# Two rows of probabilities masked at once, and seven kinds of small work handed from VectorE to GpSimd

## Chip, cores and metric

The kernel runs on one core of one Trainium2 chip. The metric is the device time of one execution in microseconds; below, that is the median of three runs. The engines are named as in the profile: PE is TensorE's matmul, PEld its weight load, DVE is VectorE, ACT is ScalarE, POOL is GpSimd, SP is SyncE, which here only issues DMAs.

## What is computed

A transformer layer in float32: x is 8 batches of 1024 rows of 128 features. After a layer norm comes attention with 8 heads of 16 features and relative positions, whose scores are shifted, and then a router with eight experts, two per token. Cut to what matters here:

```python
content = jnp.einsum('bqhd,bkhd->bhqk', q + u_bias, k)
pos_score = jnp.einsum('bqhd,khd->bhqk', q + v_bias, p)
pos_score = _rel_shift(pos_score)          # pad one column, reshape, drop the first row
score = (content + pos_score) / jnp.sqrt(jnp.float32(e))
attn = jax.nn.softmax(score, axis=-1)
ctx = jnp.einsum('bhqk,bkhd->bqhd', attn, v).reshape(b, s, e)
x = x + ctx @ Wo + bo
...
router_logits = jnp.einsum('bsk,ke->bse', h, Wr2) + br2     # then top 2 of 8 experts
output = output + y * expert_mask[:, :, e][:, :, None]      # for each expert
```

The shift makes three kinds of score for a query row and a key column. On and below the diagonal one set of operands holds ("lower", QL), from two above the diagonal on another ("upper", QU), and on the super-diagonal, one above, the position part is absent. So a 128x128 block on the diagonal is a mixture.

## The kernel before, in words

The kernel has a prologue (to about 88 us), a loop over the eight batches of attention and routing (to about 1233), an end of the routing, and then the experts (from about 1312). The change touches the loop and what leads to it; of the experts only the name of one tensor's slice.

**The loop.** A batch is 8 heads of 9 units, u = 0 to 8; (h, u) names head and unit. Every engine has its own program of the same 72 units, written out by hand, and waits on counting semaphores of the others. In a unit PE does two halves of the second pass of head h (scores of one block row of 128 keys by 1024 queries, into pB, L677) and two pieces of the first pass of head h + 2 (scores into the three banks of pA, L655), which VectorE reads to find the maxima (L1083, L1089). ScalarE takes the exponentials of pB (L985, L987): at u = 0 into `upper_diag`, the diagonal blocks computed with the upper operands, at u > 0 into `prob`, a ring of four rows, kb = u - 1. GpSimd masks (L555 to L575): at u = 0 the eight upper blocks at once; at each u > 0 it sets one element to zero (L568), keeps the lower triangle of the diagonal block (L570) and adds the upper block (L575), and then counts `p_mask` by one. PE's `context` (L698) waits for that count; it runs for two rows at a time, at units 4, 6 and 8 for rows 0 to 5 and at unit 1 of the next head for rows 6 and 7.

**Work between the units.** Tables such as `LOW_AT` name the unit at which a piece of other work is done. Float32 operands are split into a high half, rounded, and a low half, the rest; c, k, gl and gu are the operands, each in two pieces of 512 columns, for the next batch. ScalarE makes the high halves, VectorE the low ones (`low`, L1062), each counted in `low_done`. gu is read from PSUM, c, k and gl from SBUF. SyncE stores them to DRAM at heads 2, 3 and 4 (`store`, L291). `maxima` (L1093) ends a head on VectorE: it reduces the maxima to `mneg` and makes `dsup`, the difference on the super-diagonal, of which ScalarE takes the exponential at the head's end (L1029). The other small work on VectorE's path in this text is the normalization of the values (`vsh`, L1117 to L1127, head 0), the router's rows (L1155, L1158, units 0, 1, 3 and 4 of head 3, transposed by PE at L748) and its hidden layer (`hr`, L1182, units 1 and 2 of head 5, transposed by PE at L760, the "fold"). GpSimd has besides the masks the position products (L482 to L491), reciprocal roots (L453 to L469, L505, L507), the residual's bias (L497) and the indirect DMAs that scatter routed rows (L517).

**Order.** Nothing is planned by a program: each engine's queue is in the order of its code, and these tables set where the small work stands in it. The mask's core is

```python
if kb > 0:
    po.memset(prob[kb % RING][0:1, P * kb - 1:P * kb], 0.0)
p = prob[kb % RING][:, P * kb:P * kb + P]
po.affine_select(out=p, in_=p, compare_op=ALU.is_ge, fill=0.0, base=0,
                 pattern=[[1, P]], channel_multiplier=-1).then_inc(lower_masked, 1)
```

Of the kernel before, what the change touches and what calls it, by code (L numbers as in the profile page):

```python
# [21 lines left out]
P = 128  # L22
# [47 lines left out]
def attention_phase(nc, dram, keep):  # L70

    ctx = ExitStack()
    with ctx:
# [36 lines left out]
        prob = [keep["b2"]] + [sb(f"prob{i}", [P, S]) for i in range(1, RING)]  # L110
# [50 lines left out]
        ln, low_done, pos, norm, rs_done, res_done = (sem(n) for n in ("ln", "low_done", "positions", "norm", "rs_done", "residual_biased"))  # L161
# [12 lines left out]
        LN_N, LOW_N, POS_N, NORM_N, HI_N, RS_N = 3 * NB, 8, 8, 6, 8, 9  # L174
# [23 lines left out]
        LOW_AT = {(1, 2): 0, (2, 3): 1, (2, 7): 2, (3, 2): 3, (3, 6): 4, (4, 1): 5, (4, 3): 6, (4, 4): 7}  # L198
        POSITIONS_AT = ((1, 1), (1, 4), (1, 8), (2, 1), (2, 4), (2, 6), (5, 4), (5, 6))
# [4 lines left out]
        RESIDUAL_AT, LAST_HEADS_AT, FIRST_HEADS_AT = ((7, 1), (7, 4)), (0, 6), (6, 4)  # L204
# [4 lines left out]
        SCATTER_AT = ((0, 1), (0, 4), (0, 6), (0, 8), (1, 6), (3, 1), (3, 6), (3, 8), (4, 4), (4, 6), (5, 1), (5, 8), (6, 1), (6, 4), (6, 6), (6, 8))  # L209
# [44 lines left out]
        def _(sp):  # L254
# [145 lines left out]
            sp.dma_start(keep["b2"][:, :], dram["b2"].partition_broadcast(P)).then_inc(d_big, 16)  # L400
# [14 lines left out]
        def _(po):  # L415
# [5 lines left out]
            for i in range(1, RING):  # L421
                po.memset(prob[i][:, :], 1.0).then_inc(set_pool, 1)
# [69 lines left out]

            def residual(b, half):
# [40 lines left out]
            for i in range(RS_N):  # L534
# [15 lines left out]
                             pattern=[[1, P]], channel_multiplier=-1).then_inc(set_r, 1)  # L550
            po.wait_ge(m_done, 1)
# [491 lines left out]
        def _(v):  # L1043
# [255 lines left out]
            for n in range(4, LOW_N):  # L1299
                low(0, n)  # L1300
# [452 lines left out]
```

## Time and profile before

| | us |
|---|---|
| median of three runs | 1685.92 |
| lowest, highest run | 1685.19, 1691.73 |
| the profiled execution, as a run | 1683.95 |
| its span in the trace | 1682.2 |

The rows further down come from this one execution. Their times are microseconds from the span's start. "xN" is a count, "idle before" or a bracket at a row's end is the time for which the engine did nothing before the instruction and what released it. Matmuls are pipelined and their ends are modelled: a row of PE of 0.40 us does not mean that the next cannot start after 0.23. Weight loads (PEld) run ahead of their matmuls. `b_all` in a row is the ring's first row, which lies in the tensor of an expert bias (`b2`).

### The profile page before, as it was taken

What the parts mean: (1) busy time and instruction counts of PE and PEld (TensorE: products, weight loads), DVE (VectorE), ACT (ScalarE), POOL (GpSimd) and SP (SyncE); (2) the same over time, 40 slices, a digit from 0 to 9 for tenths busy, and PEclk for the clock granted to TensorE, in tenths of its full rate; (3) what the DMA queues carried; (4) which work ended last, traced back from release to release, by engine and by line L of the source; (5) the groups of instructions that cost most, each with busy time, mean ns of one, the idle gap of its engine ahead of it and who ended that gap; (6) DMA issues with size and microseconds to landing.
All of it is one profiled execution on the core that took longest, in us unless ns stands there. A gap on an engine that the chain in (4) does not pass through costs nothing. (4 is left out here: it accounts for less than half of the span.)

```text
span 1682.2 us, 51020 instructions
## 1 busy us (share of the span) xinstructions
PE 1549.5 (92%) x12534; PEld 1207.6 (72%) x12535; DVE 1402.2 (83%) x5272; ACT 1113.2 (66%) x2303; POOL 1106.0 (66%) x2090
## 2 busy tenths in 40 slices
PE   3789999999999999999999999999951799999997
PEld 1567777677676767777767776767731799999997
DVE  4669899989989987998998998899854588888886
ACT  2157776776777776677777777767730577777775
POOL 5257767767766775776677677677663276666666
PEclk8689999999999998999999999999975899999999
DMA  5746535535644553464364355346454243443433
GB/s 136 198 116 177 145 94 156 163 93 130 183 111 122 163 155 85 104 198 108 104 185 136 96 160 164 97 122 189 113 147 127 43 59 52 56 57 51 57 53 48
DMA packets 134404, 199.99 MB, mean 119 GB/s; under 512 B 20936, under 2 KB 95576, under 8 KB 134192
## 3 DMA queue, kind: packets, MB, share of 16 engines
q1 hardware_dynamic: 108336, 177.21, 39.1%
q0 software_dynamic: 25856, 20.27, 7.8%
q8 instruction: 94, 1.54, 0.4%
q14 instruction: 118, 0.97, 0.2%
HBM read 108.24 MB, written 75.33 MB: 109 GB/s over the span
## 5 line engine op out<-in xcount | busy, mean ns | idle before, releaser
L1083 DVE CUSTOM_DVE_ANT_0 junk<-pA,lmask 128x512 bf16<-128x512 f32 x1056 | 686.8, 682 | 63.1 <-PE pA L670 44.1
L985 ACT ACTIVATE prob<-pB 128x512 f32<-128x512 f32 x384 | 229.9, 599 | 204.5 <-PE pB L689 115.8
L1576 POOL DMA_INDIRECT out<-yb,dst x144 | 230.9, 1604 | 134.9 <-ACT yb L1650 82.5
L691 PE MATMUL pB<-QL,K 97*128 97x512 f32 (+3 forms) x768 | 285.7, 372 | 1.4 <-ACT upper_diag L985 1.4
L668 PE MATMUL pA<-K,QL 96*128 96x512 f32 (+3 forms) x792 | 281.8, 357 | 5.0 <-DMA K<-split_operands 3.2
L689 PE MATMUL pB<-QU,K 97*128 97x512 f32 (+3 forms) x640 | 267.1, 417 | 0.3
L670 PE MATMUL pA<-K,QU 96*128 96x512 f32 (+3 forms) x660 | 233.1, 354 | 4.5 <-DVE acc L1083 3.2
L987 ACT ACTIVATE prob<-pB 128x512 f32<-128x512 f32 x384 | 227.8, 593 | 12.7 <-PE pB L691 4.5
L707 PE MATMUL pC<-prob,vext 128*17 128x256 f32 x3088 | 217.4, 384 | 0.1
L575 POOL TENSOR_TENSOR prob<-prob,upper_diag 128x128 f32<-128x128 f32 x384 | 180.2, 469 | 32.0
L689 PEld LDWEIGHTS pB<-QU,K 97*128 97x128 f32 x640 | 121.9, 190 | 99.4 <-issue 59.3
L517 POOL DMA_INDIRECT routed_rows<-sent,sent_to x144 | 157.9, 1097 | 29.9 <-issue 25.6
L568 POOL MEMSET prob<- 1x1 f32 x384 | 34.0, 89 | 203.9 <-ACT prob L987 202.6
L668 PEld LDWEIGHTS pA<-K,QL 96*128 96x128 f32 x792 | 153.5, 194 | 13.8 <-DVE acc L1083 4.4
L1089 DVE CUSTOM_DVE_ANT_0 junk<-pA,umask 128x128 bf16<-128x128 f32 x528 | 122.1, 284 | 43.8 <-PE pA L674 41.3
L691 PEld LDWEIGHTS pB<-QL,K 97*128 97x128 f32 x768 | 147.1, 192 | 15.8 <-ACT upper_diag L985 3.3
L1689 DVE SCALAR_TENSOR_TENSOR g<-pLin,b_all,gl 128x256 f32<-128x256 f32 x292 | 127.5, 478 | 22.6 <-PE pLin L1599 14.5
L670 PEld LDWEIGHTS pA<-K,QU 96*128 96x128 f32 x660 | 128.0, 194 | 22.2 <-DVE acc L1083 14.9
L1605 PE MATMUL pY<-w_all,g 128*128 x1152 | 140.3, 275 | 0.0
L707 PEld LDWEIGHTS pC<-prob,vext 128*17 128x17 f32 x3088 | 78.1, 97 | 84.0 <-issue 22.3
L1605 PEld LDWEIGHTS pY<-w_all,g 128*128 128x128 f32 x1152 | 135.0, 192 | 0.0
L1643 ACT ACTIVATE gl<-pGate,b_all 128x256 f32<-128x256 f32 x292 | 121.0, 465 | 13.1 <-PE pGate L1599 12.2
(305 smaller groups left out, 3656.5 us busy)
## 6 DMA issues: line engine op xcount, KB each, us to landing
QL<-split_operands SPq DMA_DIRECT2D x67, 256.0 KB, 3.7
QU<-split_operands SPq DMA_DIRECT2D x67, 256.0 KB, 4.1
K<-split_operands SPq DMA_DIRECT2D x67, 256.0 KB, 4.4
xg<-routed_rows SPq DMA_DIRECT2D x76, 132.0 KB
split_operands<-c_h SPq DMA_DIRECT2D x36, 256.0 KB, 6.1
split_operands<-c_l SPq DMA_DIRECT2D x36, 256.0 KB, 6.4
QL<-split_operands SPq DMA_DIRECT2D x67, 128.0 KB, 3.6
QU<-split_operands SPq DMA_DIRECT2D x67, 128.0 KB, 4.1
```

Of the source, the lines that this page charges most:

```text
L517: po.indirect_dma_start(dram["xs"], bass.IndirectOffsetOnAxis(sent_to[:, t, j:j + 1], 0), sent[:, t, :], None).then_inc(scattered, 16)
L575: po.tensor_tensor(p, p, upper_diag[h % 2][:, P * kb:P * kb + P], ALU.add).then_inc(p_mask, 1)
L668: mm = pe.matmul(dst[:, 0:low], QL[0:KROWS, s, q], K[0:KROWS, s, k0:k0 + low], start=True, stop=True)
L670: mm = pe.matmul(dst[:, low:HALF], QU[0:KROWS, s, q], K[0:KROWS, s, k0 + low:k0 + HALF], start=True, stop=True)
L689: mm = pe.matmul(pB[:, q0:q0 + up], K[0:r, s, k], QU[0:r, s, q0:q0 + up], start=True, stop=True)
L691: mm = pe.matmul(pB[:, q0 + up:q0 + HALF], K[0:r, s, k], QL[0:r, s, q0 + up:q0 + HALF], start=True, stop=True)
L707: mm = pe.matmul(pC[VW * strip:VW * strip + D + 1, :], vext[:, kb, h % H, :], prob[kb % RING][:, quarter * strip:quarter * strip + quarter ...
L985: act.activation(p[:, 0:HALF], pB[:, 0:HALF], ACT.Exp, scale=SCALE).then_inc(p_exp, 1)
L987: act.activation(p[:, HALF:S], pB[:, HALF:S], ACT.Exp, scale=SCALE).then_inc(p_exp, 1)
L1083: v.tensor_tensor_reduce(out, src[:, :], lmask[:, at:at + HALF], 1.0, -3.0e38, ALU.add, ALU.max, acc[:, s, qb, n % 2:n % 2 + 1]).then_inc( ...
L1576: po.indirect_dma_start(dram["out"], bass.IndirectOffsetOnAxis(dst[k][:, a:a + 1], 0), yb[k][:, a, :], None, compute_op=ALU.add).then_inc( ...
L1605: mm = pe.matmul(pY[k % 2][:, a, :], g[k % 2][:, c, P * a:P * a + P], keep["w2"][:, bass.ds(ex * F + c * E, E)], start=(c == 0), stop=(c = ...
```

## The change

The ring of four rows becomes two tensors of two rows each. GpSimd no longer masks a row at every unit u > 0, but two rows at the even units: one select over both diagonal blocks and one addition over both, and `p_mask` rises by two. Six of the eight low halves per batch (c, k and gl) and the eight differences `dsup` move from VectorE to GpSimd; the two of gu, which lie in PSUM, stay, with a semaphore of their own (`gu_low`). The differences stand at unit 3 of the head before. Positions, scatters and a residual move by a unit or so, mostly to odd units. VectorE waits for all eight differences before it overwrites the super-diagonal's scores, and PE for the six low halves before it projects into their sources.

```diff
-        prob = [keep["b2"]] + [sb(f"prob{i}", [P, S]) for i in range(1, RING)]
+        ring = [keep["b2"], sb("prob23", [P, 2, S])]
+        prob = [ring[i // 2][:, i % 2, :] for i in range(RING)]
...
-        LOW_AT = {(1, 2): 0, (2, 3): 1, (2, 7): 2, (3, 2): 3, (3, 6): 4, (4, 1): 5, (4, 3): 6, (4, 4): 7}
+        LOW_AT = {(3, 6): 4, (4, 4): 7}
+        SPLIT_AT = {(0, 3): 0, (1, 8): 1, (2, 8): 2, (3, 3): 3, (3, 7): 5, (4, 2): 6}
+        DSUP_AT = 3
...
-                sp.wait_ge(low_done, lows)
+                sp.wait_ge(gu_low if name == "gu" else low_done, lows)
...
+            def low(nb, n):
+
+                name, half = SPLITS[n]
+                cut = slice(HALF * half, HALF * half + HALF)
+                src = {"c": qu, "k": kc, "gl": g_lo}[name][:, cut]
+                have = known(po, nb * HI_N + n + 1)
+                po.wait_ge(set_pool, POOL_SET)
+                po.wait_ge(hi_done, have)
+                po.tensor_tensor(parts[name][1][:, cut], src, parts[name][0][:, cut].bitcast(F32), ALU.subtract).then_inc(low_done, 1)
+
+            def super_difference(b, h):
+
+                s = h % H
+                have = known(po, b * H + h + 1)
+                po.wait_ge(set_pool, POOL_SET)
+                po.wait_ge(mx_done, have)
+                po.tensor_tensor(dsup[:, s, :], acc[:, s, :, 3], mneg[:, s, :].bitcast(F32), ALU.add).then_inc(dsup_done, 1)
...
-                        else:
-                            kb = u - 1
-                            if kb > 0:
-                                po.memset(prob[kb % RING][0:1, P * kb - 1:P * kb], 0.0)
-                            p = prob[kb % RING][:, P * kb:P * kb + P]
+                        elif u % 2 == 0:
+                            kb = u - 2
+                            both_rows = ring[kb // 2 % 2][:, :, :].rearrange("p a s -> p (a s)")
+                            for k in (kb, kb + 1)[kb == 0:]:
+                                po.memset(prob[k % RING][0:1, P * k - 1:P * k], 0.0)
+                            p = both_rows.rearrange("p (n q) -> p n q", q=P)[:, kb:kb + NB + 2:NB + 1, :]
                             po.affine_select(out=p, in_=p, compare_op=ALU.is_ge, fill=0.0, base=0,
-                                             pattern=[[1, P]], channel_multiplier=-1).then_inc(lower_masked, 1)
+                                             pattern=[[0, 2], [1, P]], channel_multiplier=-1).then_inc(lower_masked, 1)
...
-                            po.tensor_tensor(p, p, upper_diag[h % 2][:, P * kb:P * kb + P], ALU.add).then_inc(p_mask, 1)
+                            po.tensor_tensor(p, p, upper_diag[h % 2][:, P * kb:P * kb + 2 * P].rearrange("p (n q) -> p n q", q=P), ALU.add).then_inc(p_mask, 2)
+                        if u == DSUP_AT:
+                            super_difference(b, h + 1)
+                        if (h, u) in SPLIT_AT:
+                            low(b + 1, SPLIT_AT[h, u])
...
+                                    pe.wait_ge(low_done, (b + 1) * LOW_N + LOW_N)
...
-                v.wait_ge(mx_done, b * H + h + 1)
-                v.tensor_tensor(dsup[:, s, :], acc[:, s, :, 3], mneg[:, s, :].bitcast(F32), ALU.add).then_inc(dsup_done, 1)
...
                 elif name == "super":
+                    v.wait_ge(dsup_done, b * H + H)
                     super_out(src, done)
```

How this moves instructions is best seen in the queues. First GpSimd, from the end of head 2 to the start of head 3: `prob` and `b_all` are rows of the ring, `rs_r` the router's reciprocal root, `upper_diag` the upper blocks. Before:

```order
L575 TENSOR_TENSOR prob<-prob,upper_diag 128x128
L62 ISA
L505 TENSOR_SCALAR rs_r<-mv_r 128x8
L507 TENSOR_TENSOR rs_r<-rs_r,mhalf 128x8
L62 ISA
L568 MEMSET prob 1x1
L570 AFFINE_SELECT prob<-prob 128x128
L572 REGISTER_ALU
L575 TENSOR_TENSOR prob<-prob,upper_diag 128x128
L62 ISA
L563 AFFINE_SELECT upper_diag<-upper_diag 128x1024
```

and with the change:

```order
L602 TENSOR_TENSOR b_all<-b_all,upper_diag 128x2x128
L62 ISA x2
L530 TENSOR_SCALAR rs_r<-mv_r 128x8
L532 TENSOR_TENSOR rs_r<-rs_r,mhalf 128x8
L62 ISA
L595 MEMSET prob 1x1 x2
L597 AFFINE_SELECT prob<-prob 128x2x128
L599 REGISTER_ALU
L602 TENSOR_TENSOR prob<-prob,upper_diag 128x2x128
L508 TENSOR_TENSOR k_l<-kc,k_h 128x512
L62 ISA
L589 AFFINE_SELECT upper_diag<-upper_diag 128x1024
```

The mask of the seventh row no longer stands ahead of the root, and the first low half of k now stands between the last mask and the select of the next head's upper blocks.

Second VectorE, around unit 2 of head 3: `junk` with `lmask` is the read of a score bank. Before:

```order
L62 REGISTER_ALU
L1083 ISA junk,acc<-pA,lmask 128x512
L1083 ISA acc 128x1
L1067 REGISTER_ALU
L1068 TENSOR_TENSOR k_l<-kc,k_h 128x512
L62 REGISTER_ALU
L1083 ISA junk,acc<-pA,lmask 128x512
L1083 ISA acc 128x1
L62 REGISTER_ALU
L1083 ISA junk,acc<-pA,lmask 128x512
L1083 ISA acc 128x1
L1158 SCALAR_TENSOR_TENSOR rows_r<-xres,mv_r,rs_r 128x128 x2
```

and with the change:

```order
L62 REGISTER_ALU
L1116 ISA junk,acc<-pA,lmask 128x512
L1116 ISA acc 128x1
L62 REGISTER_ALU
L1116 ISA junk,acc<-pA,lmask 128x512
L1116 ISA acc 128x1
L62 REGISTER_ALU
L1116 ISA junk,acc<-pA,lmask 128x512
L1116 ISA acc 128x1
L1189 SCALAR_TENSOR_TENSOR rows_r<-xres,mv_r,rs_r 128x128 x2
```

The low half of k is gone from between the reads, and the router's third step stands right behind them.

Third GpSimd at units 3 and 4 of head 0. Before, with the ring's rows numbered:

```order
L62 ISA
L568 MEMSET prob2 1x1
L570 AFFINE_SELECT prob2<-prob2 128x128
L572 REGISTER_ALU
L575 TENSOR_TENSOR prob2<-prob2,upper_diag0 128x128
L62 ISA
L568 MEMSET prob3 1x1
L570 AFFINE_SELECT prob3<-prob3 128x128
L572 REGISTER_ALU
L575 TENSOR_TENSOR prob3<-prob3,upper_diag0 128x128
L517 DMA routed_rows<-sent,sent_to 67584x132
```

and with the change:

```order
L516 TENSOR_TENSOR dsup<-acc,mneg 128x8
L62 ISA
L508 TENSOR_TENSOR c_l<-qu,c_h 128x512
L62 ISA
L595 MEMSET prob23 1x1 x2
L597 AFFINE_SELECT prob23<-prob23 128x2x128
L599 REGISTER_ALU
L602 TENSOR_TENSOR prob23<-prob23,upper_diag0 128x2x128
```

A difference and the first low half of c take the place of a mask at unit 3, the pair is masked at unit 4, and the scatter behind it has moved to unit 5.

## Rows read from the trace of the kernel before

**Rows 1.** The page: busy time, share of the span and instructions.

```profile
PE 1549.5 (92%) x12534; PEld 1207.6 (72%) x12535; DVE 1402.2 (83%) x5272; ACT 1113.2 (66%) x2303; POOL 1106.0 (66%) x2090
```

**Rows 2.** Windows: stretch, length, busy of five engines (instructions), TensorE clock, DMA share, GB/s.

```profile
797.70:939.20 141.50, 139.99 (x1159) 100.25 (x1157) 129.08 (x530) 103.87 (x211) 100.68 (x232) 1.00 0.49 136
...
630.00:635.00 5.00, 5.00 (x31) 4.25 (x29) 3.26 (x15) 3.00 (x7) 2.60 (x7) 0.82 0.26 69
635.00:640.00 5.00, 5.00 (x28) 3.19 (x28) 2.97 (x19) 2.07 (x4) 2.26 (x7) 0.50 0.04 14
```

**Rows 3.** Waits of weight loads, 797.7 to 939.2: us in total, times, longest.

```profile
PEld pM L760 <- DVE hr L1182: 1.4, 1, 1.4
PEld pA L670 <- DVE acc L1083: 1.1, 3, 0.5
...
PEld pM L748 <- DVE rows_r L1158: 0.7, 1, 0.7
...
PEld pM L734 <- DVE vsh L1127: 0.3, 1, 0.3
PEld pA L668 <- DVE acc L1083: 0.3, 1, 0.3
```

**Rows 4.** Timeline, batch 5: start, us, instruction, count, idle before and releaser.

```profile
833.65 0.19 PEld L668 LDWEIGHTS pA<-K,QL 96*128 96x128 f32 x1 [0.30 <-DVE acc L1083]
...
867.38 0.20 PEld L748 LDWEIGHTS pM<-ident_f,rows_r 128*128 128x128 f32 x2 [0.20 <-issue]
...
872.13 0.42 PEld L748 LDWEIGHTS pM<-ident_f,rows_r 128*128 128x128 f32 x4 [0.72 <-DVE rows_r L1158]
...
904.08 0.42 PEld L760 LDWEIGHTS pM<-ident_f,hr 128*128 128x128 f32 x4 [1.35 <-DVE hr L1182]
```

**Rows 5.** VectorE's lines that move: ns minimum/median/maximum, first and last start.

```profile
L1068 DVE TENSOR_TENSOR c_l<-qu,c_h x18: 677/810/991, 30.2 to 1134.6; 128x512 fp32r<-128x512 f32 x18
L1068 DVE TENSOR_TENSOR k_l<-kc,k_h x18: 673/676/686, 31.6 to 1150.7; 128x512 fp32r<-128x512 f32 x18
L1068 DVE TENSOR_TENSOR gl_l<-g_lo,gl_h x18: 673/682/689, 41.1 to 1169.3; 128x512 fp32r<-128x512 f32 x18
...
L1099 DVE TENSOR_TENSOR dsup<-acc,mneg x66: 166/189/650, 71.2 to 1233.1; 128x8 f32<-128x8 f32 x66
```

**Rows 6.** GpSimd's nearest forms, from the answers on single lines, as above.

```profile
L570 POOL TENSOR_SCALAR_AFFINE_SELECT prob<-prob x384: 282/293/819, 99.7 to 1232.5; 128x128 f32<-128x128 f32 x192
...
L575 POOL TENSOR_TENSOR prob<-prob,upper_diag x384: 453/458/1332, 100.1 to 1232.9; 128x128 f32<-128x128 f32 x192
...
L491 POOL TENSOR_TENSOR g_lo<-g_lo,t x18: 1259/1282/1287, 35.2 to 1140.4; 128x512 f32<-128x512 f32 x18
```

**Rows 7.** Timeline around the start of head 3: GpSimd, then VectorE, then PE.

```profile
859.08 0.88 POOL L575 TENSOR_TENSOR prob<-prob,upper_diag 128x128 f32<-128x128 f32 x1
...
860.38 1.67 POOL L507 TENSOR_TENSOR rs_r<-rs_r,mhalf 128x8 f32<-128x8 f32 x1
...
862.43 0.46 POOL L575 TENSOR_TENSOR prob<-prob,upper_diag 128x128 f32<-128x128 f32 x1
862.84 1.10 POOL L563 TENSOR_SCALAR_AFFINE_SELECT upper_diag<-upper_diag 128x1024 f32<-128x1024 f32 x1
...
862.88 1.09 DVE L1155 TENSOR_SCALAR rows_r<-rows_r 128x8 f32<-128x8 f32 x1
863.88 0.71 DVE L1158 SCALAR_TENSOR_TENSOR rows_r<-xres,mv_r,rs_r 128x128 f32<-128x128 f32 x2
...
863.19 1.06 PE L707 MATMUL pC<-prob,vext 128*17 128x256 f32 x16
```

**Rows 8.** Timeline, head 0 of the same batch: VectorE and GpSimd.

```profile
812.23 1.22 DVE L1117 TENSOR_TENSOR vsh<-vsh,psup 128x1024 f32<-128x1024 f32 x1
...
812.42 1.35 POOL L575 TENSOR_TENSOR b_all<-b_all,upper_diag 128x128 f32<-128x128 f32 x1 [0.17 <-POOL b_all L570]
...
817.55 1.29 DVE L1119 TENSOR_TENSOR vsh<-vsh,ctx_all 128x896 f32<-128x896 f32 x1
```

More of the change, by code:

```diff
@@ L160, in attention_phase @@
         e_ready, e_done, hi_done = sem("e_ready"), sem("e_done"), sem("hi_done")
-        ln, low_done, pos, norm, rs_done, res_done = (sem(n) for n in ("ln", "low_done", "positions", "norm", "rs_done", "residual_biased"))
+        ln, low_done, gu_low, pos, norm, rs_done, res_done = (sem(n) for n in ("ln", "low_done", "upper_low", "positions", "norm", "rs_done", "residual_biased"))
         placed, moved = sem("head_values_placed"), sem("values_shifted")
@@ L171, in attention_phase @@
         block = ctx.enter_context(nc.Block())
-        LN_N, LOW_N, POS_N, NORM_N, HI_N, RS_N = 3 * NB, 8, 8, 6, 8, 9
+        LN_N, LOW_N, GU_N, POS_N, NORM_N, HI_N, RS_N = 3 * NB, 6, 2, 8, 6, 8, 9
         E_AT = [1, 2, 4, 6, 7, 8, 9, 10]
@@ L229, in attention_phase @@
         READY = {"c": 2, "k": 4, "gl": 7, "gu": 8}
+        LOWS = {"c": 2, "k": 4, "gl": 6}
         PAIRS_AT = {1: (-1, 6), 4: (0, 0), 6: (0, 2), 8: (0, 4)}
@@ L315, in _ @@
                 sp.wait_ge(hi_done, READY[name])
-                sp.wait_ge(low_done, READY[name])
+                if name == "gu":
+                    sp.wait_ge(gu_low, GU_N)
+                else:
+                    sp.wait_ge(low_done, LOWS[name])
                 store_side(name, 0)
@@ L399, in _ @@
             sp.dma_start(keep["b1"][:, :], dram["b1"]).then_inc(d_big, 16)
[L400 removed]
+            sp.dma_start(keep["b2"][:, 0, :], dram["b2"].partition_broadcast(P)).then_inc(d_big, 16)
             sp.wait_ge(w_done, B * W_N + 2)
@@ L421, in _ @@
             for i in range(1, RING):
-                po.memset(prob[i][:, :], 1.0).then_inc(set_pool, 1)
+                po.memset(prob[i], 1.0).then_inc(set_pool, 1)
             po.memset(mhalf[:, :], -0.5).then_inc(set_pool, 1)
@@ L550, in _ @@
                              pattern=[[1, P]], channel_multiplier=-1).then_inc(set_r, 1)
+            super_difference(0, 0)
             po.wait_ge(m_done, 1)
@@ L723, in _ @@
             pe.wait_ge(low_done, LOW_N)
+            pe.wait_ge(gu_low, GU_N)
             for h in range(AHEAD):
@@ L787, in small_piece @@
                 elif part == 0 and name == "values 0":
-                    pe.wait_ge(low_done, (b + 1) * LOW_N + LOW_N)
+                    pe.wait_ge(gu_low, (b + 1) * GU_N + GU_N)
                 elif part == 0:
@@ L848, in _ @@
                                 else:
-                                    pe.wait_ge(low_done, (b + 1) * LOW_N + SPLITS.index(("gu", 0)) + 1)
+                                    pe.wait_ge(gu_low, (b + 1) * GU_N + 1)
                                 upper_form(half, pE, 0, 2)
@@ L1298, in _ @@
                 stats(1, t)
-            for n in range(4, LOW_N):
+            for n in range(4, HI_N):
                 low(0, n)
@@ L1712, in step @@
                 v.wait_ge(down, i + 1)
-                v.tensor_tensor(yb[k][:, :, :], pY[k % 2][:, :, :], keep["b2"][:, bass.ds(step.experts[k] * E, E)].unsqueeze(1).to_broadcast([P, HALVES, E]), ALU.add).then_inc(y_done, 1)
+                v.tensor_tensor(yb[k][:, :, :], pY[k % 2][:, :, :], keep["b2"][:, 0, bass.ds(step.experts[k] * E, E)].unsqueeze(1).to_broadcast([P, HALVES, E]), ALU.add).then_inc(y_done, 1)
             ex = load_experts(mybir.EngineType.DVE, 0, 2)
```

14 lines of the change are left out of this document (7 added, 7 removed).

## The prediction, as it was put on record

> **What bounds the kernel now.** I read the page's busy line first, then one batch of the loop by window, then who waited for whom in that batch, then single stretches of the timeline. The page says PE 92%, VectorE 83%, GpSimd 66% [rows 1]. The change touches only the eight-batch loop, so one batch has to be read: batch 5, from 797.70 to 939.20 us, 141.50 us long, with VectorE busy 129.08, PE 139.99, ScalarE 103.87 and GpSimd 100.68 us at full TensorE clock [rows 2]. The next batch is as long to the hundredth; one row stands for all.
>
> VectorE at 91% looks like the bound, and then every microsecond taken from it would be a microsecond of time. The waits say otherwise. Weight loads run just ahead of their matmuls, so idle time before a weight load is the plainest sign that PE is held up. In the whole batch VectorE held weight loads up for 1.4 (router fold), 1.1 and 0.3 (score banks not yet read), 0.7 (router rows) and 0.3 (values): 3.8 us of 141.5, seven times [rows 3]. Elsewhere PE goes on with its own queue, or plays ping-pong with ScalarE's exponentials, whatever VectorE does. So VectorE has a backlog in places, three score banks deep, which mostly costs nothing. **The change can give back at most those 3.8 us per batch, and only those whose backlog contains a removed instruction.**
>
> **What is taken from VectorE.** Per batch two low halves each of c (810 ns median), k (676) and gl (682), and eight differences of 189 ns [rows 5]: 2 x (0.81 + 0.68 + 0.68) + 8 x 0.19 = 5.9 us, 47 us in eight batches. Now each held-up place:
> - Head 1, the score bank at 833.65, held up 0.30 [rows 4]. Two units ahead of it VectorE did a low half of c (up to 991 ns [rows 5]), with no idle time from there to the read that frees the bank. That goes. The wait can lose 0 to 0.30; I take 0.15, since a load also idles for its issue.
> - Head 3, router rows at 872.13, held up 0.72 [rows 4]. The low half of k at head 3, unit 2, stands two router steps ahead of it. It is worth 0.68, more than the wait beyond the 0.20 that the same line idles where it waits for nothing (867.38) [rows 4]. Gain 0.52.
> - Head 5, router fold at 904.08, held up 1.35 [rows 4]. VectorE works without a gap from the end of head 4; of its work there only one difference goes. Gain 0.19.
> - The other four (two more banks in head 3, one in head 2, the normalized values at the start of head 1) stand before a removed low half, or behind an idle gap of VectorE that swallows the removed difference: 0.
> - The low halves of gl in head 4 and the second of c and the first of k in head 2 stand where nobody waits: 0.
>
> Relief: 0.15 + 0.52 + 0.19 = 0.86 us per batch, **6.9 us in eight** (bounds: 0 if other backlogs move in; 8 x 1.01 = 8.1 if the 0.30 goes whole).
>
> **What GpSimd gets.** A fused mask covers 2 x 128 columns. The trace has no such form; the nearest rows are select 0.29 us for 128 columns and 1.10 for 1024, addition 0.46 for 128 and 1.28 for 512 [rows 6, 7]. By straight lines between them, an estimate: 0.40 and 0.73. A pair cost 2 x (0.29 + 0.46) = 1.50 and now costs 1.13, so four pairs and eight heads save 0.37 x 32 = 11.8 us per batch, less a little for the access pattern. The six low halves cost 6 x 1.28 = 7.7 by the same 128x512 addition, the eight differences between 0 and 8 x 0.46 = 3.7. So GpSimd stays at about 100 us of 141.5: load is no danger.
>
> Latency could be. A pair is masked only once its second row is there, and then takes 0.38 longer than one row did (1.13 against 0.75). The contexts consume a pair two units later, and the scarcest place I found in the batch is head 3, unit 1: mask done at 862.89, contexts at 863.19, 0.30 to spare [rows 7]. There the new order is no later: the row masked ahead of the root (0.88 for its addition alone) goes, so the root's power starts near 859.1 instead of 860.38 and the pair is done near 862.1. Elsewhere the pair has 0.6 us or more. I take 0; once, at the loop's very end, 0.4 us. The moved positions, scatters and the residual now lie mostly at odd units, which have no mask any more: hidden in that room. New waits on PE and VectorE (the differences before the super-diagonal is overwritten, the low halves before the projection) are met three units or more ahead: 0. SyncE's stores of c, k and gl wait for GpSimd's halves one or two units later than for VectorE's, but are needed heads later: 0.
>
> **What the two engines do to each other** is the cost I cannot read straight off. An addition of GpSimd that is 458 ns in the median took 1.35 us at 812.42, beside a two-input VectorE operation of 1.22 us from 812.23 [rows 6, 8]. In the other direction a 128x8 step of VectorE took 1.09 us at 862.88, beside a 1.10 us select of GpSimd from 862.84 [rows 7], and the low half of c ranges from 677 to 991 ns [rows 5]. So they do not overlap freely: the later one waits. Not always, though: at 863.88 two VectorE steps took 0.71 us beside GpSimd work, nearly undelayed [rows 7]. The Trainium skill says more sharply (SBUF — State Buffer, section "Who interferes with whom") that a VectorE instruction with two SBUF inputs and a GpSimd instruction that reads SBUF exclude each other for the whole of whichever came first. By that rule the trace agrees in its long overlaps and not in this short one.
>
> Two places are exposed. Head 3, unit 0: by the durations above GpSimd would do pair, low half of k (862.1 to 863.4) and then the select (to 864.5), where the router step of 863.88 ended at 864.59. That step could end up to 0.6 later, and the two bank waits of head 3 behind it are without slack. Head 0, unit 4: the VectorE operation at 817.55 [rows 8] meets the pair's addition of 0.73, where it met one of 0.46; it may win or lose by a tenth, 0 to 0.7, and VectorE has no gap from there to the values that ScalarE and PE wait for. Bounds: 0 to 1.3 per batch. I take 0.3, near the lower end, as the short overlaps of the trace cost 0.1 to 0.2 each: **+2.4 us in eight**.
>
> **Sum.** -6.9 + 2.4 + 0.4 = -4.1 us. The profiled execution took 1683.95, so 1679.9; the median of the runs lies 1.97 above it (1685.92), so 1681.8 us, 0.24% less.
>
> **The rivals.**
> A. *VectorE is the bound after all.* For it: 91% busy, and PE's 99% proves little, since the ends of its matmuls are modelled. The Trainium skill (Perfetto Trace Analysis, section "Identifying the Most-Contended Engine") ranks engines by occupancy and takes VectorE's as a fair measure, but PE's only by its weight loads; by that rule VectorE would come first here. Against it: 3.8 us of held-up loads. Then all 47 us come back: 1639. Chance 0.05.
> B. *Relief without a price.* GpSimd's operations fall beside single-input work of VectorE, and ScalarE's ping-pong gains a little too. 1685.92 - 8.1 + 0.4 = 1678.2; and the traced execution has one stretch at half clock within the loop (granted 0.82 over 630 to 635 and 0.50 over 635 to 640, which is 1.2 GHz, though PE shows no idle time in either [rows 2]), some 13 us long, which cost at most half of that; without it 6 us less, 1672. Chance 0.25 for under 1677.5.
> C. *The port takes more than it gives.* Each low half holds VectorE's two-input work at head 0 and head 3, 1.3 us per batch, and the relief of 0.86 is used up by the same delay, which reaches the router rows: 1685.92 + 8 x 1.3 + 0.4 = 1696.7. It ends slower once the two places cost more than the relief by 1 us per batch. For it: overlaps of 0.9 us in the rows; against: GpSimd may well start before VectorE arrives, and the trace's usual overlaps cost little. Chance 0.15, counting milder forms joined by a second stretch at half clock.
> D. The forecast, 1677.5 to 1694: chance 0.55.
>
> **How the numbers follow.** The range should reach from B's lower value to the milder part of C: 1671 to 1693. What lies beyond is A and the whole of C, about 0.2. Half a per cent, 8.4 us, is about what a measurement of this kernel can tell from no change: faster 0.30 (A and B), within 0.55, slower 0.15.
>
> **What would show it.** In the profile after: VectorE's busy time in a batch near 123 us, GpSimd's near 100, and the batch near 141.0. The held-up load of the router rows gone, that of the fold near 1.15, the bank waits of head 3 unchanged or up to 0.6 longer. VectorE's idle time before score banks grows by some 6 us per batch: that is where the freed time goes. Wrong if the batch is under 139 (then backlog counted everywhere), if the fused select or addition takes over 1 us, or if contexts wait for GpSimd by more than 0.4 anywhere.

## The result, and the profile after

The changed kernel is slower: 1703.89 us (median of 5 runs, 1699.0 to 1706.83) against 1690.35 for the kernel before (5 runs beside them and earlier, 1685.19 to 1693.68), ratio 1.0086, 95% interval 1.0063 to 1.0108. The profiled execution took 1706.2 us, 22.3 more than that of before. Its page:

```profile
PE 1560.8 (92%) x12534; PEld 1213.0 (71%) x12535; DVE 1370.5 (80%) x5158; ACT 1113.4 (65%) x2303; POOL 1074.7 (63%) x1691
```

VectorE has lost 32 us of busy time and GpSimd 31 against [rows 1], and PE needed 11 more. So work was saved on both engines and time was lost. Windows of one batch, cut at VectorE's maxima so that each is one head (stretch, length, busy of PE, weight loads, VectorE, ScalarE, GpSimd, granted clock, DMA share, GB/s): heads 0, 3, 4, 6 and the whole, first of before (batch of [rows 2], cut 10.6 us later), then of after.

```profile
808.33:826.59 18.26, 18.26 (x148) 13.22 (x146) 17.10 (x57) 13.06 (x27) 13.19 (x29) 1.00 0.48 125
...
860.89:878.74 17.85, 17.45 (x140) 11.88 (x139) 16.84 (x62) 13.51 (x26) 13.64 (x33) 1.00 0.66 199
878.74:897.80 19.06, 19.04 (x164) 14.24 (x161) 16.66 (x71) 13.25 (x29) 14.50 (x35) 1.00 0.64 185
...
914.63:933.80 19.17, 19.17 (x170) 14.74 (x166) 15.91 (x82) 13.87 (x29) 12.82 (x30) 1.00 0.34 90
...
808.33:949.88 141.55, 140.04 (x1160) 100.25 (x1158) 129.14 (x529) 103.92 (x212) 100.73 (x231) 1.00 0.49 136
```

```profile
820.62:839.44 18.82, 18.50 (x146) 13.10 (x145) 17.37 (x57) 12.92 (x26) 13.08 (x23) 1.00 0.46 125
...
873.08:891.74 18.66, 17.79 (x144) 12.30 (x142) 17.09 (x61) 13.67 (x28) 15.08 (x30) 1.00 0.65 198
891.74:911.12 19.38, 19.14 (x163) 14.24 (x161) 15.18 (x69) 13.25 (x29) 13.16 (x28) 1.00 0.60 178
...
928.00:947.58 19.58, 19.58 (x168) 14.84 (x166) 16.06 (x81) 14.17 (x30) 11.10 (x23) 1.00 0.33 87
...
820.62:963.66 143.04, 140.14 (x1159) 100.23 (x1158) 125.34 (x516) 103.94 (x211) 96.38 (x181) 1.00 0.49 135
```

A batch is 1.5 us longer, 12 in eight, in four heads; the undisturbed batches of before lie between 141.43 and 141.58 us, those of after between 142.99 and 143.10, which makes a batch's length a far finer measure than the whole time. In heads 0 and 3 VectorE is busier than before although instructions were taken away there: its busy time holds waiting. The weight loads held up by VectorE in that batch (us, times, longest) answer to [rows 3]:

```profile
PEld pM L792 <- DVE hr L1213: 1.5, 1, 1.5
...
PEld pA L699 <- DVE acc L1116: 0.8, 2, 0.4
PEld pA L701 <- DVE acc L1116: 0.8, 1, 0.8
...
PEld pM L780 <- DVE rows_r L1189: 0.6, 1, 0.6
PEld pM L766 <- DVE vsh L1158: 0.6, 1, 0.6
PEld pM L805 <- DVE both L1249: 0.4, 1, 0.4
```

Sum 4.7. The same count for before gives 4.0: the prediction's 3.8 left out one wait of 0.2 for `both` (L1218). GpSimd's new operations cost what was estimated (groups by form: busy us, mean ns; the mean of an addition holds its waiting, its median is 0.73 us):

```profile
L602 POOL TENSOR_TENSOR prob<-prob,upper_diag 128x256 f32<-128x256 f32 x128 | 99.8, 780 | 19.0
...
L597 POOL TENSOR_SCALAR_AFFINE_SELECT prob<-prob 128x256 f32<-128x256 f32 x128 | 52.3, 408 | 0.0
...
L508 POOL TENSOR_TENSOR c_l<-qu,c_h 128x512 fp32r<-128x512 f32 x16 | 20.6, 1285 | 0.0
...
L516 POOL TENSOR_TENSOR dsup<-acc,mneg 128x8 f32<-128x8 f32 x65 | 13.7, 211 | 42.5 <-DVE mneg L1130 24.2 <-ACT prob L1020 17.6
```

The rest of the 22.3 us lies in stretches at half clock (2.8 in the last batch), in batch 0 (2.0), ahead of the loop (2.6), behind it (2.1) and in the experts (0.5). The two stretches outside the loop look like chance: kernels with the same prologue as the changed one reached the loop's start between 82.0 and 87.0 us (before 83.4, after 86.0), and the end part took 79.6 to 83.6 us over fourteen traces (before 81.5, after 83.6, the longest).

### The profile page after: what moved, and what is told of

Same layout as the page of the kernel before. It is cut to its first block and busy times, and to the rows that moved or that the text cites. A ratio compares the mean times of both kernels' runs of the same rounds, so it can differ in the third digit from the quotient of the medians.

```text
span 1704.5 us, 50588 instructions
## 1 busy us (share of the span) xinstructions
PE 1560.8 (92%) x12534; PEld 1213.0 (71%) x12535; DVE 1370.5 (80%) x5158; ACT 1113.4 (65%) x2303; POOL 1074.7 (63%) x1691
## 5 line engine op out<-in xcount | busy, mean ns | idle before, releaser
L1608 POOL DMA_INDIRECT out<-yb,dst x144 | 235.6, 1636 | 130.7 <-ACT yb L1682 77.1
L1018 ACT ACTIVATE b_all<-pB 128x512 f32<-128x512 f32 x256 | 153.1, 598 | 146.8 <-PE pB L720 81.4
L1018 ACT ACTIVATE prob<-pB 128x512 f32<-128x512 f32 x256 | 153.4, 599 | 115.8 <-PE pB L720 61.7
L1020 ACT ACTIVATE prob<-pB 128x512 f32<-128x512 f32 x256 | 151.8, 593 | 9.6 <-PE pB L722 4.2
L1020 ACT ACTIVATE b_all<-pB 128x512 f32<-128x512 f32 x256 | 152.1, 594 | 4.9 <-PE pB L722 1.7
L738 PE MATMUL pC<-prob,vext 128*17 128x256 f32 x2064 | 138.2, 386 | 1.0 <-POOL prob L602 1.0
L738 PE MATMUL pC<-b_all,vext 128*17 128x256 f32 x2048 | 138.0, 388 | 0.9 <-POOL b_all L602 0.9
```

Of the source, the lines that this page charges most:

```text
L738: mm = pe.matmul(pC[VW * strip:VW * strip + D + 1, :], vext[:, kb, h % H, :], prob[kb % RING][:, quarter * strip:quarter * strip + quarter ...
L1018: act.activation(p[:, 0:HALF], pB[:, 0:HALF], ACT.Exp, scale=SCALE).then_inc(p_exp, 1)
L1020: act.activation(p[:, HALF:S], pB[:, HALF:S], ACT.Exp, scale=SCALE).then_inc(p_exp, 1)
L1608: po.indirect_dma_start(dram["out"], bass.IndirectOffsetOnAxis(dst[k][:, a:a + 1], 0), yb[k][:, a, :], None, compute_op=ALU.add).then_inc( ...
```

## Where each piece of it is

Timeline (start, us, instruction). Head 0, unit 6, the addition of the last head's values on VectorE and GpSimd's mask beside it, before and after:

```profile
821.77 0.31 DVE L1121 TENSOR_TENSOR vsh<-vsh,ctx_all 128x128 f32<-128x128 f32 x1
...
821.47 0.46 POOL L575 TENSOR_TENSOR prob<-prob,upper_diag 128x128 f32<-128x128 f32 x1
```

```profile
833.92 0.79 DVE L1152 TENSOR_TENSOR vsh<-vsh,ctx_all 128x128 f32<-128x128 f32 x1
...
833.83 0.73 POOL L602 TENSOR_TENSOR b_all<-b_all,upper_diag 128x256 f32<-128x256 f32 x1
```

Both end 0.15 after GpSimd's addition: 821.93 to 822.08 before, 834.56 to 834.71 after. The fused addition is longer, so the wait is. It happens again at unit 8:

```profile
837.91 1.61 DVE L1158 TENSOR_TENSOR vsh<-vsh,den 128x1024 f32<-128x1024 f32 x1
...
837.71 0.73 POOL L602 TENSOR_TENSOR prob<-prob,upper_diag 128x256 f32<-128x256 f32 x1
```

Head 3: the low half of k (874.75 to 876.04) holds the first router step, and pushes the select behind it onto the next two, which last 1.51 together where the same two took 0.71 [rows 7]:

```profile
875.46 0.61 DVE L1186 TENSOR_SCALAR rows_r<-rows_r 128x8 f32<-128x8 f32 x1
875.99 1.51 DVE L1189 SCALAR_TENSOR_TENSOR rows_r<-xres,mv_r,rs_r 128x128 f32<-128x128 f32 x2
...
874.75 1.29 POOL L508 TENSOR_TENSOR k_l<-kc,k_h 128x512 fp32r<-128x512 f32 x1
876.00 1.10 POOL L589 TENSOR_SCALAR_AFFINE_SELECT upper_diag<-upper_diag 128x1024 f32<-128x1024 f32 x1
```

Head 6, end: a copy of 8 columns, 0.21 us before, ends with GpSimd's addition (947.18):

```profile
946.50 0.71 DVE L1245 COPY rows_r<-xf 128x8 f32<-128x8 f32 x1
...
946.45 0.73 POOL L602 TENSOR_TENSOR prob<-prob,upper_diag 128x256 f32<-128x256 f32 x1
```

Head 4 looked like more of the same, a scatter in the way, and was not (below). The working theory P: each instruction of GpSimd holds a VectorE instruction that needs the same access until it ends. Rival L: masks and differences come later, contexts or exponentials wait. Later came C: breaks in VectorE's own supply of instructions, seen as an instruction that starts late although its wait is met and no other engine holds it.

## The experiments

Each head is the third smallest of its seven lengths (batch 0 left out), so that stretches at half clock drop out (for head 6 of e5 and e10 the second smallest); sum is their sum. Head 0 of e5, e10 and e12 does not repeat as the others do (19.00 to 19.51, 19.13 to 19.78 and 18.57 to 19.19 us), so their sums are low by some tenths. Ratio is the whole time against the kernel before on the same chip.

| kernel | h0 | h1 | h2 | h3 | h4 | h5 | h6 | h7 | sum | ratio, 95% |
|---|---|---|---|---|---|---|---|---|---|---|
| before | 18.26 | 18.00 | 16.27 | 17.85 | 19.05 | 16.80 | 19.16 | 16.08 | 141.5 | |
| after | 18.81 | 17.77 | 15.86 | 18.64 | 19.38 | 16.87 | 19.58 | 16.07 | 143.0 | 1.0063 to 1.0108 |
| e1 | 18.17 | 17.77 | 15.89 | 18.61 | 19.42 | 16.89 | 19.62 | 16.07 | 142.4 | 1.0025 to 1.0072 |
| e2 | 18.81 | 17.78 | 15.89 | 17.69 | 19.42 | 16.88 | 19.62 | 16.07 | 142.2 | 1.0016 to 1.0065 |
| e3 | 18.81 | 17.77 | 15.86 | 18.63 | 19.39 | 16.88 | 19.58 | 16.07 | 143.0 | 1.0036 to 1.0080 |
| e4 | 18.17 | 17.77 | 15.86 | 17.69 | 19.39 | 16.88 | 19.45 | 16.08 | 141.3 | 0.9977 to 1.0010 |
| e5 | 19.17 | 17.77 | 15.89 | 17.68 | 19.07 | 17.19 | 19.18 | 16.09 | 142.0 | 1.0038 to 1.0086 |
| e6 | 18.81 | 17.76 | 16.79 | 17.35 | 19.06 | 16.94 | 19.64 | 16.07 | 142.4 | 1.0029 to 1.0077 |
| e7 | 18.35 | 17.78 | 15.87 | 19.23 | 19.38 | 16.63 | 19.45 | 15.95 | 142.6 | 1.0032 to 1.0071 |
| e8 | 18.26 | 17.77 | 15.89 | 17.41 | 19.06 | 16.78 | 19.16 | 16.08 | 140.4 | 0.9868 to 0.9939 |
| e9 | 18.17 | 17.76 | 15.86 | 17.68 | 19.37 | 16.88 | 19.21 | 16.22 | 141.2 | 0.9987 to 1.0043 |
| e10 | 19.30 | 17.78 | 15.87 | 17.69 | 19.40 | 17.18 | 19.14 | 16.08 | 142.4 | a single run |
| e11 | 18.17 | 17.76 | 15.86 | 17.67 | 19.02 | 16.89 | 19.21 | 16.22 | 140.8 | 0.9945 to 0.9971 |
| e12 | 18.62 | 18.00 | 16.27 | 18.17 | 19.04 | 16.61 | 19.19 | 16.45 | 142.3 | 0.9999 to 1.0030 |

**e1.** Two of the 32 pairs masked row by row again, with a select and an addition of 128 columns each, as before the change:

```diff
+        SINGLE_AT = ((0, 6), (0, 8))
...
+                        elif (h, u + u % 2) in SINGLE_AT:
+                            kb = u - 1
...
```

> The changed kernel, but the two last pairs of rows of head 0 (units 5 to 8) are masked row by row as before; all other pairs stay fused. Theory P (GpSimd's longer addition holds VectorE's two-input steps): in the changed kernel the addition of values at unit 6 of head 0 waits for a fused addition of 0.73 us (0.79 us instead of 0.31), and the last one at unit 8 for another (1.61 instead of 1.36). Both go back, PE's held-up score bank at the end of head 0 (+0.36) and the late values at the start of head 1 (+0.27) with them: a batch 143.0 -> 142.3 us, the whole 5 to 6 us less than the changed kernel. Theory L (the loss is latency: contexts or exponentials wait for the later masks or for GpSimd's queue): two of 32 pairs matter little, at most 0.1 us per batch.

Head 0 fell 0.64, no other moved by more than 0.04. P stands for head 0; L doesn't.

**e2.** `-(2, 8): 2, (3, 3): 3` `+(3, 3): 3, (3, 5): 2` in SPLIT_AT.

> The changed kernel, but GpSimd makes the first low half of k at unit 5 of head 3, not at unit 8 of head 2, so that the select of the upper blocks is not pushed back by 1.28 us. Theory P: the router step at the start of head 3 lasts 0.45 us again, not 1.25, and the two score banks behind it come 0.3 and 0.25 us earlier: a batch 143.0 -> 142.5. Theory L: no more than 0.1, since nobody waits for the low half of k. If something at units 5 and 6 of head 3 is hit instead, the batch stays at 143.0 and the new delay shows there.

Head 3 fell 0.95, almost twice what was expected. P again.

**e3.** `-(3, 5), (4, 5), (4, 7)` `+(3, 5), (4, 4), (4, 7)` in SCATTER_AT.

> The changed kernel, but one of the sixteen scatters, that of head 4, unit 5, is issued at unit 4, as before the change. Theory P, widened to GpSimd's indirect DMAs: in the changed kernel the four short score reads of unit 6 in head 4 start 0.44 us after their wait is over, just as the scatter ends, and PE is held up 0.36 us at unit 8; that goes: a batch 143.0 -> 142.65. Theory L or chance: the batch stays within 0.1 us of 143.0.

Nothing moved: head 4 keeps its 19.39, and the late reads with it, with GpSimd idle beside them. P widened to scatters fails: the scatter had only stood there.

**e4.** e1, e2 and e3 together, SINGLE_AT with (6, 8) too.

> The changed kernel with all three repairs, and the last pair of head 6 masked row by row too (there a copy of the router's choice lasted 0.71 us instead of 0.21 beside the fused addition, 0.29 us late at head 7). Theory P: 143.0 - 0.7 - 0.5 - 0.35 - 0.3 = 141.15 us per batch, below the kernel before (141.48) by the 0.3 us of relief, and the whole about 15 us under the changed kernel, 0 to 3 us under the kernel before. Theory L: 142.5 or more per batch.

141.3 instead of 141.15: heads 0 and 3 add up, head 6 gave only 0.13, head 4 nothing. The whole is level with the kernel before, as the batch says (-0.17 x 8 = -1.4 us).

**e5.** e4, and in VectorE's loop:

```diff
+                        if (h, u) == (1, 6):
+                            for _ in range(20):
+                                v.wait_ge(set_dve, DVE_SET)
```

> The kernel with all repairs (141.31 us per batch), with 20 waits that are always met (0.02 us each) put into VectorE's program at head 1, unit 6, where it idles 0.8 us: as many instructions as the change took out of VectorE's program ahead of head 4. What stayed late in all variants, the short score reads of head 4, unit 6 (they start 0.44 us after their wait is met, with GpSimd idle; 0.08 elsewhere), hits always the same instruction, 491st of the 871 of the loop. Theory C (a break in VectorE's supply of instructions, at a fixed distance in its program): the break moves to another instruction and head 4 lasts 19.05 us again, as before the change: 141.31 -> 140.95, unless the new place is as bad. Theory S (something that head 4 itself does, whatever stands ahead): nothing moves, 141.3.

Ten more instructions stand in the loop (881 for 871; waits are paired). Head 4 fell to 19.07, three heads further on than the padding: theory C. But head 0 rose by 1.0 and head 5 by 0.3, and the sum is 142.0. Head 0 is a break behind the loop's branch (e12). Head 5 is a small break that lets GpSimd go first: a short read comes 0.15 us late, the fused addition starts at 915.25, 0.07 ahead of VectorE's step with `rq`, and that step lasts 1.21 us; in e4 the step started 0.11 ahead of the addition and lasted 0.69, and the addition waited.

**e6.** SPLIT_AT empty, all eight lows in VectorE's LOW_AT, the differences back in `maxima`.

> The changed kernel with the six low halves and the eight differences back on VectorE at their old places: of the change only the fused masks and the moved positions, scatters and residual are left. Theory P: the fused addition costs 0.55 at head 0 and about 0.3 at head 6 by itself, so with no relief left a batch is 141.48 + 0.9 = 142.4, and GpSimd is busy only about 88 us of it. Theory L (GpSimd's queue and its added work delay the masks): the cost came with the added work, so 141.5 or less.

142.4 as expected by P, with VectorE busy 130 us and GpSimd only 89. The fused masks cost 0.55 at head 0; of the 0.48 at head 6 about half belongs to a moved scatter (e9). Head 2 is 0.5 longer, which was not expected, and it is P again, this time by a moved position product of GpSimd that meets the low half of c left on VectorE (0.75 us before the change in the same batch):

```profile
853.73 1.62 DVE L1098 TENSOR_TENSOR c_l<-qu,c_h 128x512 fp32r<-128x512 f32 x1
...
853.52 1.28 POOL L498 TENSOR_TENSOR g_lo<-g_lo,t 128x512 f32<-128x512 f32 x1
```

Head 3 is 0.5 shorter: the mask of the seventh row no longer stands ahead of the select of the upper blocks, the select starts 0.4 us earlier in the head, and the router steps wait less for it.

**e7.** SINGLE_AT holds all 32 pairs.

> The changed kernel with all rows masked one by one as before: of the change the low halves and differences on GpSimd and the moved tables are left. GpSimd then has about 108 of 143 us busy. Theory P: without the fused additions 0.55 and 0.3 go, the delay by the low half of k (0.8) and the late reads of head 4 (0.36) stay: 142.1. Theory L: GpSimd's queue is longer than in the changed kernel, so contexts wait: 143.5 or more.

142.6: between the two. Heads 0 and 6 behave as P says, and head 5 falls by 0.24, since an addition of 128 columns holds a step of `hr` for 0.47 us instead of 0.75. Head 3 is 0.6 worse than in the changed kernel: masks one by one shift GpSimd's queue, and the second low half of k now meets a router step (the first of the two below lasts 1.28):

```profile
872.28 1.54 DVE L1205 SCALAR_TENSOR_TENSOR rows_r<-xres,mv_r,rs_r 128x128 f32<-128x128 f32 x2
...
872.13 1.28 POOL L510 TENSOR_TENSOR k_l<-kc,k_h 128x512 fp32r<-128x512 f32 x1
```

GpSimd is busy 107.7 us of it, and no head but the third is longer than in the changed kernel: its load alone costs nothing that shows.

**e8.** In the kernel before:

```diff
-                cut = slice(HALF * half, HALF * half + HALF)
+                cut = slice(HALF * half, HALF * half + (HALF if isinstance(nb, int) or name == "gu" else 8))
```

> The kernel before, with the six low halves of c, k and gl cut to 8 columns inside the loop (0.1 us instead of 0.7 to 0.8; the rest of the computation of these halves is left out): the relief alone, with nothing put on GpSimd. The prediction's terms for it: 0.15 at head 1 and 0.52 at head 3, 141.48 -> 140.8. Theory N (VectorE's backlog hides it all, the freed time turns into idle time ahead of the next score bank): 141.4. Theory V (VectorE is the bound): 4 us less, 137.5.

140.4: the relief by six low halves is 1.05 us per batch, 0.23 in head 1, 0.38 in head 2, 0.44 in head 3. V is far off, N too. The profiled execution is 12.0 us shorter than that of before: 8.4 by the batches, 6.2 by a stretch of 13.7 us at half clock that is missing (batch 3 of before 147.71, its neighbours 141.48), less 1.5 each for two stretches of 3.4 us. The ratio of the runs says 16 us; what makes the rest is not shown.

**e9.** `SPLIT_AT = {(0, 3): 0, (1, 8): 1, (3, 5): 2, (3, 7): 3, (4, 1): 5, (4, 2): 6}`, SINGLE_AT as e4, scatter (6, 7) to (6, 8).

> The changed kernel with the two last pairs of head 0 and the last of head 6 masked row by row, and moved on GpSimd: both low halves of k to head 3, units 5 and 7, behind the router steps of that head (the first low half of gl follows at head 4, unit 1), and the scatter of head 6, unit 7, to unit 8, behind the mask that it holds up in the repaired kernel. Theory P: head 3 lasts 17.41 us as in the kernel with short low halves, not 17.69, and head 6 lasts 19.16 as before the change, not 19.44: 141.31 -> 140.75 us per batch, 0.7 below the kernel before, 6 us in eight. If the two-input steps of other places are hit by the moved low halves: 141.3 or more.

Head 6 came as expected (19.21). Head 3 did not move: the second low half of k had held nobody. Why e8's head 3 is 0.27 shorter is seen in e11 below. The whole time does not show the gain: the interval holds 1, and the runs reach from 1679.8 to 1702.8 us.

**e10.** e5's padding at (4, 7) instead of (1, 6).

> The kernel with all repairs, with the same 20 waits that are always met (10 instructions in the trace), but at head 4, unit 7, behind the late reads. Theory C (breaks in VectorE's supply of instructions at fixed distances in its program): the instructions up to head 4 stand where they stood, so the reads of head 4, unit 6 are late again (19.4 us for head 4, where 10 instructions ahead of them gave 19.07), and what comes behind them, head 5 (17.19 instead of 16.88) and head 6 (20.4 instead of 19.44), is as with the other padding. Theory S: head 4 as with the other padding or all as without.

Head 4 is 19.40 again, head 5 as with the other padding, and head 0 long again (19.30): C, since nothing but the position differs. Head 6 is 19.14 and not 20.4: that expectation had taken a stretch at half clock in e5 for a break. Head 6 of e5, then of e10 (last but two: granted clock):

```profile
919.01:939.74 20.73, 20.73 (x165) 15.12 (x164) 15.92 (x81) 13.69 (x30) 11.32 (x24) 0.92 0.31 80
```

```profile
921.89:941.03 19.14, 19.14 (x165) 14.54 (x164) 15.91 (x81) 13.70 (x30) 11.33 (x24) 1.00 0.33 87
```

**e11.** e9 with `range(4)` at (1, 6): two more instructions.

> The kernel with the low halves of k moved behind the router steps, with 4 waits that are always met (2 instructions in the trace) at head 1, unit 6. Theory C: the break in VectorE's supply, that stood at instruction 491, right behind an idle stretch of 1.0 us, then falls ahead of that stretch and is swallowed by it: head 4 19.05 us instead of 19.37, a batch 141.16 -> 140.85, unless two instructions are enough to bring on the breaks at the loop's start and in heads 5 and 6 that ten instructions brought (then 141.8 or more). Theory S: 141.16.

140.8, as C said, and the fastest version that computes everything: 1684.09 us, 0.9958 of the kernel before (0.9945 to 0.9971). That is 6.7 us, of which the batches account for 5.2 (0.65 in each); the padding itself gave 0.34 per batch against e9, and the larger difference between the whole times of e9 and e11 is mostly not its doing. The place in question, VectorE's read of four products of PE, in the changed kernel and in e11:

```profile
904.96 0.29 DVE L1122 CUSTOM_DVE_ANT_0 junk<-pA,umask 128x128 bf16<-128x128 f32 x1 [1.48 <-PE pA L705]
...
903.90 0.56 PE L705 MATMUL pA<-K,QU 96*128 96x128 f32 x4
```

```profile
888.30 0.29 DVE L1138 CUSTOM_DVE_ANT_0 junk<-pA,umask 128x128 bf16<-128x128 f32 x1 [1.12 <-PE pA L721]
...
887.59 0.56 PE L721 MATMUL pA<-K,QU 96*128 96x128 f32 x4
```

The products end at 904.46 and 888.15; the read follows 0.50 us later in one, 0.15 in the other. The wait is named in both, and only the lag behind it tells.

In the same trace head 3 shows what is left of its loss. A fused addition holds the first of two router steps for 0.73 us; in e8, with additions of 128 columns, that step took 0.38:

```profile
867.80 0.99 DVE L1205 SCALAR_TENSOR_TENSOR rows_r<-xres,mv_r,rs_r 128x128 f32<-128x128 f32 x2
...
867.64 0.73 POOL L618 TENSOR_TENSOR prob<-prob,upper_diag 128x256 f32<-128x256 f32 x1
```

In batch 0 of e9 and e11 the two router steps go first (0.60 us for both), the addition lasts 1.25, and head 3 takes 17.41 us as in e8. So the 0.27 left in head 3 is P as well, by one more fused addition.

**e12.** In the kernel before, `super_difference` on GpSimd at u == 3 and the difference gone from `maxima`.

> The kernel before, with the eight differences moved to GpSimd, unit 3 of each head, and nothing else. It makes VectorE 8 x 0.19 us shorter per batch and its program by some 20 instructions. The prediction gave the differences 0.19 us per batch, at head 5 (16.81 -> 16.6). Theory N (no wait ends on a difference): 141.48 within 0.1. Theory C adds that the shorter program may bring a break at another place of it, seen as a head that is 0.3 us or more longer with GpSimd idle: then 141.8 or more.

142.3: eight small steps less on VectorE, and a batch 0.9 us longer. Head 5 is 0.19 shorter. Head 0 is 0.36 longer and head 7 0.37, at the start and the end of VectorE's loop. Head 3 is 0.32 longer, and that is not a break but P: in before VectorE's second router step started ahead of GpSimd's addition, which waited (0.56 us); in e12 the addition comes 0.09 us earlier in the head, within 0.02 us of that step, and goes first; the step lasts 0.63 instead of 0.34 (the two together 1.00 instead of 0.71 [rows 7]). GpSimd's addition in before, then both in e12:

```profile
864.35 0.56 POOL L575 TENSOR_TENSOR b_all<-b_all,upper_diag 128x128 f32<-128x128 f32 x1 [0.16 <-POOL b_all L570]
```

```profile
877.37 1.00 DVE L1167 SCALAR_TENSOR_TENSOR rows_r<-xres,mv_r,rs_r 128x128 f32<-128x128 f32 x2
...
877.76 0.46 POOL L584 TENSOR_TENSOR b_all<-b_all,upper_diag 128x128 f32<-128x128 f32 x1
```

The whole time alone would not show a loss (ratio 1.0015, 0.9999 to 1.0030). The loop's start in e12 and in e4:

```profile
823.79 0.69 DVE L1094 CUSTOM_DVE_ANT_0 junk<-pA,lmask 128x512 bf16<-128x512 f32 x1 [2.30 <-PE pA L681]
...
821.48 0.39 PE L681 MATMUL pA<-K,QU 96*128 96x384 f32 x1
```

```profile
820.00 0.69 DVE L1132 CUSTOM_DVE_ANT_0 junk<-pA,lmask 128x512 bf16<-128x512 f32 x1 [0.75 <-PE pA L717]
...
819.47 0.39 PE L717 MATMUL pA<-K,QU 96*128 96x384 f32 x1
```

In e12 the product was ready at 821.87 and read 1.92 us later; in e4 0.14 later. VectorE's rows without data work (DVEq) show where the time goes: between the loop's branch and the record behind it, neither of which waits for a semaphore. In e12, then in e4 (ns minimum/median/maximum, first and last start):

```profile
L1326 DVEq COMPARE_BRANCH  x1: 68/68/68, 821.4 to 821.4; - x1
L1326 DVEq BRANCH_PREFETCH_HINT  x1: 39/39/39, 823.5 to 823.5; - x1
```

```profile
L1364 DVEq COMPARE_BRANCH  x1: 68/68/68, 819.2 to 819.2; - x1
L1364 DVEq BRANCH_PREFETCH_HINT  x1: 39/39/39, 819.7 to 819.7; - x1
```

From the branch's end to the next record it is 0.44 to 0.51 us in every pass of eleven kernels, and 1.6 to 2.7 us in every pass of e5, e10 and e12: C, without another engine in it, and the reason why head 0 of these three varies.

## Why the prediction was wrong

The forecast was 1681.8 (1671 to 1693); the changed kernel took 1703.9, and 13.5 us more than the kernel before. The balance per batch, against before: head 0 +0.64 by fused additions (e1), head 3 +0.95 by the low half of k (e2), head 6 +0.4 (0.13 by the fused mask, e4; 0.24 by the moved scatter in front of it, e9), head 4 +0.34 by a break in VectorE's program (e11); against that -0.23 and -0.41 in heads 1 and 2 (e8: -0.23 and -0.38) and 0.1 to 0.2 each in heads 0 and 3. Together +1.5, 12 us in eight.

- **What bounds the kernel.** Right. VectorE's busy time fell by 3.8 us per batch, the batch grew, and e8 gave 1.05, not 4.
- **Relief 0.86.** Right mechanism, near in size. Of it 0.67 was for low halves, measured 1.05. Head 1 0.15, measured 0.23. Head 3 0.52, measured 0.44. Head 2 stood at 0, since its held-up bank came before a removed low half in the listing; measured 0.38. Head 5 0.19, measured 0.19 in e12, but not in the changed kernel, where the fold waited 1.5: a fused addition in head 5 takes it back (16.87, and 16.63 with single masks, e7). The 3.8 us of held-up loads also left out 0.2 (`both`, L1218), which changes nothing.
- **Contention +0.3.** The step that failed. The bounds, 0 to 1.3, came from two exposed places, and the value from "the short overlaps of the trace cost 0.1 to 0.2 each". Measured: 0.64 + 0.95 + 0.4, about 2.0, above the upper bound, and 0.24 in head 5 and 0.27 in head 3 besides, which stayed hidden as relief that did not come. Head 3 was named with its instructions and priced at up to 0.6; the low half delayed two router steps, not one. At head 0 unit 4 was named, and units 6 and 8 cost. Head 6 was not listed; its victims are a copy with one input and, behind the moved scatter that the prediction put at nothing ("hidden in that room"), a step with two (0.56 us in e4, 0.28 in e9). And the argument from the short overlap was a misreading of [rows 7]: the select ran from 862.84 to 863.94, the two steps began at 863.88, so they had nearly nothing to wait for, and the addition that followed waited for them (0.56 us). No row that the prediction shows contradicted the rule that the later one waits to the end. Which of the two goes first can turn on less than 0.1 us (e12), and the trace before alone does not tell that for a changed queue.
- The rule that was cited with a doubt holds here for GpSimd's additions and selects, though not for its power operation (last section). The Trainium skill (SBUF — State Buffer, section "Who interferes with whom") also lists copies, casts and tensor-scalar steps of VectorE among those that can take the shared ports, and says that the loser blocks for the whole instruction; the copy above ended 0.03 us after GpSimd's addition, and the tensor-scalar step of head 3 within 0.03 of the low half's end. A count of all overlaps by that rule was not made before the run; what the forecast would have been with it is not shown.
- **Latency 0.** Right: no load of a context is put down to GpSimd in the batch. Before, 1.9 us were, but that is no gain: the loads of `context` idled 7.8 us in 24 places before (5.9 of it "issue") and 7.9 in 24 after.
- **GpSimd's load.** Estimates 0.40, 0.73, 1.28, measured 0.41, 0.73 undisturbed, 1.28. Busy 96.4 where about 100 was said, VectorE 125.3 where 123 was said: waiting counts as busy, which makes at least part of the latter.
- **Not foreseen at all:** that taking instructions out of VectorE's program shifts where it breaks. It made 0.34 of the 1.5 us, and 0.7 us in heads 0 and 7 where nothing but differences was moved (e12).
- **Chances.** Rival C (0.15) had the right mechanism and 1.3 per batch. The range took in only its milder part, though the bounds rested on two places out of all in which both engines overlap.

What stays open: what sets the distance at which VectorE's program breaks, and what brings on the stretches at half clock. Of the 42 that start in the loop over all fourteen traces 40 start in head 6, and e5 has one in six of its eight batches.

## What to carry to other kernels

When work moves to GpSimd, list every overlap of a GpSimd instruction with VectorE instructions that touch only SBUF, copies and small steps too, and price each at the rest of GpSimd's instruction (here additions and selects; the power operation held nobody); fusing two short GpSimd instructions into a longer one saves GpSimd time and lengthens those waits. Put the long ones beside VectorE's reads of PSUM, which never waited. Do the same for every piece that is only moved: a position product (e6), a low half (e2) and a scatter (e9) each cost 0.2 to 1.0 us per batch by what they or the next instruction then met. Where an engine starts an instruction 0.4 us or more after its wait is met, at the same instruction in every pass, a harmless instruction or two earlier in its program may be worth more than the edit under study.

## What the runs showed of the hardware

- VectorE instructions with two inputs in SBUF wait for the end of a two-input operation or a select that GpSimd has in progress (an addition on `vsh` took 0.79 us for 0.31), and GpSimd's wait for VectorE's in the same way (1.17 us for 0.73, e4). A copy with one input went from 0.21 to 0.71. In the trace before, all 90 such VectorE instructions that started inside such a GpSimd instruction (0.06 us or more from either end) ended after it, in the trace after all 63.
- GpSimd's power of 128x8, 1.68 us long, does not: 33 of 34 VectorE instructions that started inside one in the trace before also ended inside it, with their usual length, as in batch 0:

```profile
147.46 0.17 DVE L1099 TENSOR_TENSOR dsup<-acc,mneg 128x8 f32<-128x8 f32 x1
...
146.72 1.68 POOL L507 TENSOR_TENSOR rs_r<-rs_r,mhalf 128x8 f32<-128x8 f32 x1
```

- Score reads from PSUM are not held: of the 1056 reads of 128x512 in each of these two traces none took more than 0.69 us.
- VectorE's program breaks at places that move with its length: 0.4 us at instruction 491 of the loop's 871, gone with 2 more instructions, and 1.6 to 2.7 us from the loop's branch to the next record with 881 or 883 instructions, against 0.44 to 0.51 with 871, 873, 894 or 895. The profile puts such idle time down to the wait ahead of it.
- Undisturbed batches repeat within 0.15 us in before and after, whole executions of one kernel spread by up to 23 (e9). One cause is stretches at half clock, which come and go: one of 13.7 us costs a batch 6.2, one of 3.4 us costs 1.5.
